# A routed mixture of experts after causal attention: split products in the mixing and in part of the fold, and a new order in the last group and at the end

## The reference

```
q, k, v = mlp(x) for each, mlp(x) = gelu(x @ W1 + b1) @ W2 + b2
scores = tril(q @ k.T / sqrt(256 * 512))
x = layernorm(x + layernorm(scores @ v) * ln_w + ln_b)
xn = layernorm(x) * gamma + beta
logits = l2norm(xn) * scale @ l2norm(mu)          # tokens x 256 slots
dispatch = softmax over tokens, combine = softmax over slots
slot_in = dispatch.T @ xn
h = gelu(slot_in @ w1 + b1);  slot_out = h @ w2 + b2
x = layernorm(x + combine @ slot_out)
```

## Time and profile before

| What | Value |
|---|---|
| Median of 3 runs | 590.03 us (589.85 to 590.4) |
| The profiled execution | 590.34 us, span 588.6 us |
| Mean granted TensorE clock | 0.996 |
| Busy: PE, DVE, ACT, POOL | 97%, 83%, 67%, 67% |
| DMA | 47.04 MB, mean 80 GB/s |

### The profile page before, as it was taken

How to read it: one execution, slowest core, us unless ns; L and a number is a source line. 1 busy time by engine, 2 the same in 40 slices (tenths; PEclk the granted TensorE clock), 3 DMA queues, 4 the chain that set the end, 5 groups by cost and what they waited for, 6 DMA issues and landing times. The chain is left out here.

```text
span 588.6 us, 11698 instructions
## 1 busy us (share of the span) xinstructions
PE 572.5 (97%) x3796; PEld 528.0 (90%) x3796; DVE 485.6 (83%) x1048; ACT 393.4 (67%) x855; POOL 393.9 (67%) x395
## 2 busy tenths in 40 slices
PE   9999999999999999999999999979999999999994
PEld 7889989999999999999998999968999999888883
DVE  6579889899898898888989989979988777557885
ACT  4765666676766667667677666567688777435765
POOL 0869779789797797787977978785646443104453
PEclk9999999999999999999999999999999999999998
DMA  8324134043141331422403403105555555923445
GB/s 234 81 73 108 22 87 99 12 107 43 65 107 18 89 71 41 102 33 74 107 13 94 86 23 74 26 11 98 84 72 72 73 73 73 147 33 108 143 144 179
DMA packets 163473, 47.04 MB, mean 80 GB/s; under 512 B 139470, under 2 KB 159340, under 8 KB 163436
## 3 DMA queue, kind: packets, MB, share of 16 engines
q1 hardware_dynamic: 163424, 46.57, 36.9%
q10 hardware_dynamic: 12, 0.00, 0.0%
HBM read 21.39 MB, written 8.39 MB: 51 GB/s over the span
## 5 line engine op out<-in xcount | busy, mean ns | idle before, releaser
L523 POOL TENSOR_TENSOR h_lo<-xn_all,h_hi 128x512 fp32r<-128x512 f32 x32 | 41.4, 1295 | 68.2 <-ACT xn_all L649 67.1
L647 ACT ACTIVATE h_hi<-bank,bias_col 128x512 fp32r<-128x512 f32 x96 | 66.4, 692 | 18.8 <-PE bank L793 17.1
L791 PE MATMUL bank<-xnT_hi,w_hi 128*128 128x512 f32 x188 | 76.2, 405 | 0.0
L792 PE MATMUL bank<-xnT_lo,w_hi 128*128 128x512 f32 x188 | 74.4, 396 | 0.0
L793 PE MATMUL bank<-xnT_hi,w_lo 128*128 128x512 f32 x188 | 74.2, 395 | 0.0
L682 ACT CAST state_hi<-bank 128x512 fp32r<-128x512 f32 x57 | 33.5, 588 | 50.1 <-PE bank L926 50.1
L1608 PE MATMUL bank<-xn_all,e_tok 128*128 128x257 f32 x256 | 65.1, 379 | 0.0
L1190 DVE TENSOR_TENSOR state_lo<-bank,state_hi 128x512 fp32r<-128x512 f32 x57 | 39.4, 691 | 29.0 <-ACT state_hi L682 29.0
L1686 PE MATMUL bank<-w_sb,ET_all 128*128 128x256 f32 x256 | 55.4, 379 | 0.0
L1686 PEld LDWEIGHTS bank<-w_sb,ET_all 128*128 128x128 f32 x256 | 48.6, 190 | 6.6
L1507 ACT ACTIVATE e_tok<-bank,shift,xinv 128x256 f32<-128x256 f32 x64 | 36.1, 565 | 27.3 <-PE bank L1598 20.5
(11 more groups left out here) (202 smaller groups left out, 2081.6 us busy)
## 6 DMA issues: line engine op xcount, KB each, us to landing
x_all<-in_L_attn_x SPq DMA_DIRECT2D x16, 512.0 KB, 3.9
kT<-k_turn SPq DMA_DIRECT2D x128, 64.0 KB, 2.5
ET_all<-e_turn SPq DMA_DIRECT2D x64, 128.0 KB, 3.8
xn_all<-in_xT SPq DMA_DIRECT2D x15, 512.0 KB, 4.7
out<-xn_all SPq DMA_DIRECT2D x15, 512.0 KB, 3.0
w_sb<-in_L_ffn_w SPq DMA_DIRECT2D x2, 512.0 KB, 5.3
xn_all<-in_L_ffn_w SPq DMA_DIRECT2D x2, 512.0 KB, 6.6
xn_all<-in_xT SPq DMA_DIRECT2D x2, 256.0 KB, 3.5
```

Source lines behind the costliest of these rows:

```text
L523: pool.tensor_tensor(h_lo[:, V_SLOT, m, :], hv[:, m, :], h_hi[:, V_SLOT, m, :].bitcast(F32), ALU.subtract).then_inc(hv_split, 1)
L647: nc.scalar.activation(h_hi[:, h_slot(j, n), m, :], ps, ACT.Gelu, bias=bias(n, m))
L791: nc.tensor.matmul(ps, w[0], xs[0], start=start, stop=False, skip_group_check=shared)
L792: nc.tensor.matmul(ps, w[0], xs[1], start=False, stop=False, skip_group_check=shared)
```

## The change

In attention's last group, divide_tokens moves from GpSimd (one pass) to ScalarE (four copies with a scale, placed behind the roundings), weight_tokens and the inversion of group 0's norms move into GpSimd's closing body, and DVE takes two sums earlier and adds two output tiles later. In routing, the fourth tile of each group is folded with six f32r products: ScalarE rounds the exponentials, GpSimd splits them, and rounds and splits the token tile. All fold products are 258 columns wide. In the mixing the groups 4 to 15 (three batches, SPLIT_GROUPS) use split products: ScalarE rounds (round_e) and GpSimd splits (split_e) each group of ET_all, nine of twelve groups in routing, three in the mixing; DVE splits so. ET_hi lies over x1_all and ET_lo over ET_all, so x1 of these groups is written to DRAM and read back (spill_x1, reload_x1) into buffers that are free by then. DVE takes the first sum of the next group between the two statistics. The last group's order is new, with one of its two stores in ScalarE's queue.

```diff
         def add_beta(engine, k, q):
-            engine.wait_ge(tok_scaled, GT * k + GT)
+            if k == 1:
+                engine.wait_ge(tok_weighted, 1)
+            else:
+                engine.wait_ge(tok_scaled, GT if k == 0 else GT * k)
...
-                def divide_tokens(k, q):
-                    pool.wait_ge(x1_ready, GT * k + 3 * GT)
-                    pool.wait_ge(r2_ready, k + 3)
-                    pool.wait_ge(hv_split, 2 * GROUPS)
-                    pool.tensor_tensor(xn[q][:, :, 0:D], x1_all[:, GT * k:GT * k + GT, :],
-                                       r2_all[:, GT * k:GT * k + GT].unsqueeze(2).to_broadcast([P, GT, D]),
-                                       ALU.mult).then_inc(tok_divided, 1)
-
                 def weight_tokens(q):
-                    pool.wait_ge(tok_divided, 1)
+                    pool.wait_ge(tok_divided, GT)
                     pool.tensor_tensor(xn[q][:, :, 0:D], xn[q][:, :, 0:D],
                                        g_rows[:, :].unsqueeze(1).to_broadcast([P, GT, D]), ALU.mult
-                                       ).then_inc(tok_scaled, GT)
+                                       ).then_inc(tok_weighted, 1)
...
                 def body(g, j, ba, attend=True, project=True, settle=True, more=True):
                     a = g - 1
                     if not project:
                         split_vsum(a, 1)
+                        invert_norms(pool, 0, 0, minus_half[:, :])
+                        weight_tokens(1)
                         add_beta(pool, 1, 1)
                         return
...
-                    if not more:
-                        divide_tokens(1, 1)
-                        weight_tokens(1)
                     split_ktok(g, 0)
+                    if attend:
+                        invert_o(pool, a, 1)
                     if not more:
                         split_v(g, 0)
-                    if attend:
-                        invert_o(pool, a, 1)
                     split_ktok(g, 1)
...
-                    if not more:
-                        invert_norms(pool, 0, 0, minus_half[:, :])
...
+                def divide_tokens(k, q, tiles):
+                    for t in tiles:
+                        tile = GT * k + t
+                        nc.scalar.activation(xn[q][:, t, 0:D], x1_all[:, tile, :], ACT.Copy,
+                                             scale=r2_all[:, tile:tile + 1]).then_inc(tok_divided, 1)
...
-                        apply_z(act, a - 2, ja % 2, (0,))
+                        round_vsum(a, 1)
                         round_state(ba, i + 2, tail_hi[2])
                         round_masked(a)
-                        round_vsum(a, 1)
-                        apply_z(act, a - 2, ja % 2, (1, 2))
+                        divide_tokens(1, 1, (3,))
+                        apply_z(act, a - 2, ja % 2, (0, 1))
                         round_state(ba, i + 3, tail_hi[3])
-                        apply_z(act, a - 2, ja % 2, (3,))
+                        apply_z(act, a - 2, ja % 2, (2, 3))
...
                     round_ktok(g)
+                    if not more:
+                        divide_tokens(1, 1, (0, 1))
                     round_v(g, 0)
+                    if not more:
+                        divide_tokens(1, 1, (2,))
                     round_v(g, 1)
                     if not more:
                         round_vsum(g, 0)
...
                         if not more:
                             sum_v(g, j, 0)
+                            sum_v(g, j, 1)
+                            sum_v(g, j, 2)
+                            return
                         add_out(dve, a, 2)
                         add_out(dve, a, 3)
-                        if not more:
-                            return
...
-                    sum_v(a, ja, 1)
-                    sum_v(a, ja, 2)
+                    add_out(dve, a - 1, 2)
                     tail_state(2)
                     split_masked(a)
+                    add_out(dve, a - 1, 3)
...
+            SPLIT = (1, 2, 3)
+            FIRST = GB * SPLIT[0]
+            SPLIT_GROUPS = range(FIRST, GB * SPLIT[-1] + GB)
+            AGAIN = 2 * GB
+            x1_spill = nc.dram_tensor("x1_spill", [len(SPLIT_GROUPS), P, GT, D], F32, kind="Internal").ap()
...
+            SO_ORDER = (2, 3, 1)
+            FOLD_AT = GT - 1
+            WIDE = D + 2
...
+                def spill_x1(g):
+
+                    sp.wait_ge(tok_scaled, GT * g)
+                    sp.dma_start(x1_spill[n], x1_all[:, GT * g:GT * g + GT, :]).then_inc(x1_spilled[n % 2], 16)
...
+                def reload_x1(g):
+                    sp.dma_start(x1_again[g], x1_spill[n]).then_inc(x1_reloaded[n % 2], 16)
...
                 for g in range(GROUPS):
+                    if g + GB - 1 in SPLIT_GROUPS:
+                        spill_x1(g + GB - 1)
                     exchange_e(g)
...
+                for g in range(FIRST, AGAIN):
+                    reload_x1(g)
                 for k in range(LAST):
+                    if k + AGAIN in SPLIT_GROUPS:
+                        reload_x1(k + AGAIN)
                     sp.wait_ge(y_normed, GT * k + GT)
                     sp.dma_start(out_t[:, GT * k:GT * k + GT, :], y[k % GB][:, :, 0:D]).then_inc(stored[k % GB], 16)
...
+                sp.wait_ge(last_normed, 3)
+                sp.dma_start(out_t[:, GT * LAST + 2:GT * LAST + 4, :], y[LAST % GB][:, 2:4, 0:D]
...
+                def split_e(g):
+                    pool.wait_ge(e_rounded, g - FIRST + 1)
+                    exact = ET_all[:, g, :, :]
+                    pool.tensor_tensor(ET_lo[:, g, :, :], exact, ET_hi[:, g, :, :].bitcast(F32), ALU.subtract
+                                       ).then_inc(e_split, 1)
...
+                def split_fold_xn(k, q):
+                    if k > 0:
+                        pool.wait_ge(tile_folded, TB + GT * (k - 1) + FOLD_AT + 1)
+                    pool.wait_ge(xn_ready, k + 1)
+                    exact = xn[q][:, FOLD_AT, :]
+                    pool.tensor_copy(fold_xn_hi[:, 0:D + 1], exact).then_inc(fold_xn_rounded, 1)
+                    pool.wait_ge(fold_xn_rounded, k + 2)
+                    pool.tensor_tensor(fold_xn_lo[:, 0:D + 1], exact, fold_xn_hi[:, 0:D + 1].bitcast(F32), ALU.subtract
+                                       ).then_inc(fold_xn_split, 1)
...
+                def split_fold_e(k):
+                    pool.wait_ge(fold_e_rounded, k + 1)
+                    pool.tensor_tensor(fold_e_lo[:, :], e_tok[:, FOLD_AT, :], fold_e_hi[:, :].bitcast(F32), ALU.subtract
+                                       ).then_inc(fold_e_split, 1)
...
                 def route(b, last):
                     for q in range(GB):
+                        split_fold_xn(GB * b + q, q)
+                        split_fold_e(GB * b + q)
                         if not (last and q == GB - 1):
...
                                 invert_norms(pool, GB * b + q + 1, (q + 1) % GB, minus_half[:, :])
                         if not (last and q >= GB - 3):
                             add_beta(pool, GB * b + q + 3, (q + 3) % GB)
+                        if GB * b + q - 2 in SPLIT_GROUPS and not (last and q == GB - 1):
+                            split_e(GB * b + q - 2)
...
+                pool.wait_ge(e_split, GROUPS - GB - FIRST + 1)
...
                 for k in range(LAST):
                     add_residual(k)
                     invert_deviation(k)
+                    if 0 < k < GB:
+                        split_e(GROUPS - GB + k)
...
                     exps(b, t)
+                    if t % GT == FOLD_AT:
+                        act.wait_ge(e_ready, TB * b + t + 3)
+                        nc.scalar.copy(fold_e_hi[:, :], e_tok[:, FOLD_AT, :]).then_inc(fold_e_rounded, 1)
...
+                    if t % GT == GT - 1 and k - 3 in SPLIT_GROUPS and not (last and q == 0):
+                        round_e(k - 3)
...
+                def round_e(g):
+                    n = g - FIRST
+                    act.wait_ge(e_moved[g % 2], 16 * FOUR * (g // 2 + 1))
+                    act.wait_ge(x1_spilled[n % 2], 16 * (n // 2 + 1))
+                    nc.scalar.copy(ET_hi[:, g, :, :], ET_all[:, g, :, :]).then_inc(e_rounded, 1)
...
-                    nc.scalar.copy(so[:, n, :, :], so_ps[n][:, :].rearrange("p (s d) -> p s d", s=SB)
+                    nc.scalar.copy(so_hi[:, n, :, :] if n in SPLIT else so[:, n, :, :], so_ps[n][:, :].rearrange("p (s d) -> p s d", s=SB)
...
+                    if 0 < k < GB:
+                        round_e(GROUPS - GB + k)
...
+                yt = y[LAST % GB][:, 1, 0:D]
+                nc.scalar.activation(yt, yt, ACT.Identity, scale=rs_y[:, LAST % 2, 1:2],
+                                     bias=nm_y[:, LAST % 2, 1:2]).then_inc(y_normed, 1)
+                act.wait_ge(last_normed, 1)
+                act.wait_ge(y_normed, GT * LAST + 1)
```

(57 more changed lines are left out.)

80 lines of the change are left out of this document (64 added, 16 removed).

## The result

The changed kernel takes **607.99 us** (median of 5 runs, 607.84 to 609.42) against 590.4 us before (5 runs, 589.85 to 590.8): ratio 1.031, 95% interval [1.029, 1.032]. That is 17.6 us slower; the forecast was 7.6 slower, and its range ended at 603.

A forecast was written before the change was run, and what follows sets the result against it. TensorE bounded the kernel; after the change ScalarE and GpSimd would bound routing and DVE the mixing. 590.3 - 2.2 (attention) + 7.1 (routing) + 2.7 (mixing) = 597.9, stated as 597.6 us; range 588.7 to 603.

The forecast's parts named there:

- split_e: GpSimd's split of 1024 columns, in routing and mixing: taken as 2.3 us a pass.
- TensorE's saving is lost behind two loops: Routing and mixing: TensorE's -8.7 us come only where nothing else ends later; ScalarE, GpSimd and DVE would.
- its floor of 2.88: Mixing: TensorE's time for a split group, 2.88 us instead of 3.45; forecast as not reached.
- Routing, +7.1: Routing: 15 loops through ScalarE and GpSimd sum to 115.5 us against 108.4, so +7.1 us.
- The chain: Routing, last exponential to the next group's first: fold_e_hi on ScalarE, then fold_e_lo and inversion on GpSimd, 3.05 us.
- Spills and reloads at nothing: Routing and mixing: x1's trips to DRAM and back fit beside other DMA traffic, cost 0.
- Attention, -2.2: Last attention group: GpSimd's moved passes let v_lo end earlier and the stage with it, -2.2 us.
- every later step of the tail moves up by 2.2: Attention's end: state, rounding and split follow v_lo, which ends at 384.5 instead of 386.7.
- Mixing, +2.7: Mixing: +5.1 at group 4 from split_e, -2.0 in groups 5 to 14, -0.4 in the last; sum +2.7 us.
- the loop is then 3.25: Mixing, groups 5 to 14: DVE's loop in the new order takes 3.25 us a group, -2.0 us in all.
- The last group, -0.4: Mixing's last group: one sum already done and the shift overlapped, -0.4 us by the last variance.
- rival C: Routing, slower still: busy GpSimd and DVE slow each other, another 0.4 us a slot, 603 us; chance 0.12.

The follow-up runs named there:

- the two best versions: Kernel before plus split mixing for two batches, new sums, shift on GpSimd: 585.99 us; the same with attention's division on ScalarE before the last state rounding: 584.15 us.
- the new end alone: The kernel before with only the new order of the mixing's sums and of the last group: 590.40 us beside 590.32, ratio 1.000.
- the run with the wait: Changed kernel, but in the mixing GpSimd's add and split_e wait until VectorE has made the shift: 606.06 us, ratio 1.026.

## Why the prediction was wrong

The direction was right and so were the loops of routing and of the groups with split_e. The size was not, +17.6 for +7.6, and the two gains forecast in attention and in the late mixing groups didn't come.

- **TensorE's saving is lost behind two loops**: right. Without the fold's split routing is exactly as before, and reordering it gives 5.9 back. The mixing never reached its floor of 2.88.
- **Routing, +7.1**: the mechanism was right, the term under-sized: +10.5. The chain is 3.42 in a steady slot, not 3.05: fold_e_lo was priced at 0.64 from the row of another pass, takes 0.72 to 0.74 on its own and 0.95 when held. Slot 1 took 8.37 for 7.3 (7.9 in three other runs), since a power of invert_o (0.89) lies between fold_e_lo and xinv and wasn't counted. The second normalisation's cost fell into slots 3 and 6 (8.55, 9.80) rather than 2 and 5: together with these 1.2 more than forecast. Slots 7 to 13 took 1.8 more. Slot 14 gave back 1.0, having no next group to prepare.
- **split_e**: forecast at 2.3, measured 2.39 (mean of nine). The cast of 257 columns took 0.43 in the mean, for 0.45. The Trainium skill, "GPSIMD Engine Reference", section "Engine selection", calls one-input operations roughly line-rate, from which I had an estimate of 0.3; the trace sides with the row. round_e 1.04 in the chain's shadow: right. Removing all of it from routing gave 1.3.
- **Spills and reloads at nothing**: right in routing, shown by the run without the split fold. In the mixing the DMA share is 0.56 to 0.57 and no wait of VectorE names a reload; in the two best versions one store came 0.74 too late, once.
- **Attention, -2.2**: the step that failed is "every later step of the tail moves up by 2.2". v_lo did; the sums moved ahead of the state's split took the gap, and add_beta, pushed back by the moved weighting, held scale_tokens at the end. I had priced the sums' new place at nothing. The block ended 0.2 later by the traces (0.5 from the v_lo of the group before); the other 1.6 of the +1.8 is the low clock behind it, for which the forecast had no term and which may not stand in the median.
- **Mixing, +2.7**: three groups with split_e +5.3 (5.1). The step that failed is "the loop is then 3.25": it is 3.56, with the shift at 0.60 instead of 0.16, and 3.12 without the holding, so the rest of the loop was priced 0.13 too long. The earlier trace rows shows the shift at 0.16 because GpSimd's add started only later there, behind ScalarE's scaling. The new order alone leaves that as it is: in the new end alone the scaling still ends 0.63 us behind the power. With the split products it ends 0.46 before the power, so the add is ready at the moment when the shift is.
- **The last group, -0.4**: -0.3 in the trace (1.36 + 1.83 for 1.72 + 1.80), below what the medians can tell.

The cause common to the three misses is **rival C**, which I gave 0.12 and let act only in routing: GpSimd and VectorE hold each other. In the rows above a held VectorE operation on four columns ends 0.02 to 0.03 us behind GpSimd's pass, and one on 256 columns 0.28 behind it. Its shares: in the mixing 0.43 us in each of ten groups, shown by the run with the wait (3.13 for 3.56) and by the shift moved to GpSimd. In attention it is read from scale_tokens at 2.75, 3.52 and 4.37, with 1.3, 2.1 and 3.2 us of GpSimd's passes beside it. In routing VectorE's scale_tokens is 6.9 us longer in all, and fold_e_lo is held by 0.1 to 0.2 us in eleven slots, 2.0 in all; how much of the 3.4 us of excess is this and how much the miscounted queue of slots 1, 3 and 6 was not separated. C's own time of 603 was too low because it left out mixing and attention; its 5.6 us for routing were more than the 3.4 of excess.

The rule of the Trainium skill in "GPSIMD Engine Reference", section "Specifications" (the two engines share their interfaces, and contend where VectorE has two SBUF inputs or a two-port mode), agrees with this case: the shift and attention's token sums read two SBUF operands and are held. The turn, with one SBUF operand and beside GpSimd's passes through all of routing, has a mean of 641 ns for 633 before, and the sum from PSUM keeps its 0.48.
